# One stage for a kernel's first two layer norms, with the first one's statistics taken in the embedding

## The reference

```python
e  = concat([E_k[id_k] for k in 6 tables])          # (B, S, 96)
h0 = e @ w_eff.T + b                                # (B, S, 64)
h  = layer_norm(h0) * L0_tok_gamma + L0_tok_beta    # first norm, kept as the state
x  = (h - mean(h)) / sqrt(var(h) + 1e-5)            # second norm, input of the attention
h  = h + attention(x, Wq, Wk)
...
```

## Time and profile before

| | us |
|---|---|
| median of 3 runs | 5880.02 (5870.23 to 5885.07) |
| the profiled execution's own time | 5872.68 |
| its span in the profile | 5871.0 |
| PE / DVE / ACT / POOL busy | 4887.5 / 4618.5 / 2553.5 / 2715.3 |

### The profile page before, as it was taken

The page is one execution under the profiler, slowest core; times in us unless marked ns, Lnnn a source line. Parts: engine busy times, 40 slices in busy tenths (PEclk is TensorE's granted clock), DMA queues, the critical chain, the costliest instruction groups (busy, mean ns, idle before and its releaser), DMA issues. The chain is left out here.

```text
span 5871.0 us, 108850 instructions
## 1 busy us (share of the span) xinstructions
PE 4887.5 (83%) x39862; PEld 3314.3 (56%) x39929; DVE 4618.5 (79%) x8619; ACT 2553.5 (43%) x4620; POOL 2715.3 (46%) x3089
## 2 busy tenths in 40 slices
PE   5476977888739999998799999999993679948998
PEld 3463225665525666665677777777772228842452
DVE  7896998998568888886588888888885767767667
ACT  4353443444536666666233333333331442223332
POOL 0000001000636675885767777777775610016557
PEclk9687998999859999999799999999996889969999
DMA  0300000010221110000122222222221000030252
GB/s 19 87 1 6 8 15 34 17 30 26 82 57 18 22 27 13 2 2 9 31 41 44 44 44 44 44 44 44 44 45 21 8 2 3 3 76 22 78 129 42
DMA packets 262988, 195.45 MB, mean 33 GB/s; under 512 B 136426, under 2 KB 239763, under 8 KB 261427
## 3 DMA queue, kind: packets, MB, share of 16 engines
q1 hardware_dynamic: 189662, 132.54, 8.1%
q0 software_dynamic: 72912, 57.02, 6.8%
q10 hardware_dynamic: 12, 0.39, 0.0%
HBM read 113.55 MB, written 69.40 MB: 31 GB/s over the span
## 5 line engine op out<-in xcount | busy, mean ns | idle before, releaser
L3642 PE MATMUL edges_bank<-part_room,hot_room 128*128 128x512 f32 x6656 | 1528.6, 391 | 77.6 <-ACT XT L3665 57.2
L3642 PEld LDWEIGHTS edges_bank<-part_room,hot_room 128*128 128x128 f32 x6656 | 1249.5, 188 | 356.8 <-ACT XT L3665 69.5
L3621 POOL DMA_INDIRECT XT<-gat_node_table,edges_idx x1216 | 1203.1, 989 | 392.4 <-issue 309.6
L3665 ACT COPY XT<-edges_bank 128x512 f32<-128x512 f32 x832 | 475.6, 598 | 657.1 <-PE edges_bank L3642 565.4
L3760 DVE COPY_PREDICATED XT<-edges_tabs_p,XT 128x1024 f32<-128x1024 int32 (+7 forms) x768 | 576.7, 751 | 38.3 <-DVE edges_tabs_p L3733 7.0
L3741 DVE TENSOR_SCALAR hot_room<-edges_lanes,edges_nodes 128x512 fp32r<-128x512 f16 (+1 forms) x768 | 350.8, 518 | 171.6 <-PE edges_bank L3642 86.2
L583 POOL TENSOR_TENSOR X<-H,ln_f_mean 128x1024 f32<-128x1024 f32 x4 | 11.4, 2846 | 877.2 <-DVE ln_f_shift L620 877.2
L1915 ACT ACTIVATE GT<-attc_sc,attc_nm 128x256 f32<-128x256 f32 x1024 | 400.3, 481 | 31.0 <-DVE attc_nm L1993 31.0
L1993 DVE TENSOR_REDUCE attc_nm<-attc_sc 128x4 f32<-128x1024 f32 x256 | 313.0, 1223 | 109.2 <-PE attc_sc L1834 109.2
L1929 ACT ACTIVATE GT<-attc_sct 128x1024 f32<-128x1024 f32 x256 | 262.3, 1025 | 303.2 <-PE attc_sct L1845 303.2
L1834 PE MATMUL attc_sc<-XT,attc_tT 64*128 64x256 f32 x2048 | 295.0, 407 | 44.6 <-ACT GT L1915 44.5
(11 more groups left out here) (869 smaller groups left out, 10077.6 us busy)
## 6 DMA issues: line engine op xcount, KB each, us to landing
gat_states<-GT SPq DMA_DIRECT2D x32, 768.0 KB, 3.4
XT<-gat_node_table,edges_idx POOLq DMA_INDIRECT x1216
edges_lanes<-gat_places SPq DMA_DIRECT2D x128, 128.0 KB, 3.1
expert_pairs<-in_L_ffn_W_dram SPq DMA_DIRECT2D x48, 256.0 KB, 4.3
edges_lanes<-gat_places SPq DMA_DIRECT2D x64, 160.0 KB, 3.3
XT<-XT SPq DMA_DIRECT2D x32, 256.0 KB, 2.4
XT<-XT SPq DMA_DIRECT2D x64, 128.0 KB, 2.0
sorted_in<-stats SPq DMA_DIRECT2D x1, 5568.0 KB, 33.9
```

The costliest lines, as they stand in the source:

```text
L3621: nc.gpsimd.indirect_dma_start(out=rows[:, k, c, :], out_offset=None, in_=q.t_table, in_offset=bass.IndirectOffsetOnAxis(ap=idx[:, k, c:c ...
L3642: m = nc.tensor.matmul(banks[t][:], hot[:, (k * GROUPS + j) % 2, b, t, :], parts[:, p, b].rearrange("p u c -> p (u c)"), start=b == 0 and ...
L3665: nc.scalar.copy(fetched[:, (k * GROUPS + j) % 2, t].rearrange("p u c -> p (u c)"), banks[t][:]).then_inc(fetched_in, 1)
```

## The change

In `embed`, `measure(i)` takes `bn_stats` of the four tiles of step i into `g.stats`, two steps behind the one-hot of the same pass (LAG = 2). The call of `ln_tok` goes, and `layernorm` is replaced by one stage, `entry_norms`, with eight groups of 16 tiles:

- The first norm, in place in `g.H`: groups 1, 2, 4, 5 and 7 by ScalarE (16 activations of 128 x 64 each, `x * rstd + shift`), groups 0, 3 and 6 by VectorE in two operations.
- VectorE applies gamma and beta to every group, takes `bn_stats` of its 16 tiles, and works out moments for two groups at a time.
- The second norm, into `g.X`: groups 0 to 3 by ScalarE, 4 to 7 by VectorE.
- `xs` gets groups 0 to 5 by DMA from SyncE's queue (each 128 x 16 pieces of 64 floats, written at a pitch of 65 floats), groups 6 and 7 by ScalarE.
- TensorE transposes the groups in order 0 to 7 through four PSUM buffers. ScalarE copies out 0 to 4 and 6, VectorE 5 and 7.

```diff
@@ embed, VectorE
+                def measure(i):
+                    v.wait_ge(z_read, i + 1)
+                    for t in range(4 * i, 4 * i + 4):
+                        m = vec.bn_stats(g.stats[:, t, :], g.H[:, t, :])
+                    m.then_inc(measured, 1)
+                    if i == NI - 1:
+                        v.wait_ge(measured, NI)
...
                     if i:
                         collect(i - 1)
+                    if i >= LAG:
+                        measure(i - LAG)
                 collect(NI - 1)
-                v.wait_ge(z_read, NI)
+                for i in range(NI - LAG, NI):
+                    measure(i)
@@ the new stage, entry_norms
+    HT, QT, BUFS = 16, 32, 4
+    FIRST_ACT, FIRST_DVE = (1, 2, 4, 5, 7), (0, 3, 6)
+    THEN_ACT, THEN_DVE = (0, 1, 2, 3), (4, 5, 6, 7)
+    OUT_ACT, OUT_DVE = (0, 1, 2, 3, 4, 6), (5, 7)
+    COPY_DMA, COPY_ACT = (0, 1, 2, 3, 4, 5), (6, 7)
+    xn = g.X
...
+            def _(sp):
+                sp.dma_start(gam[:], gamma.partition_broadcast(P)).then_inc(params, 16)
+                sp.dma_start(bet[:], beta.partition_broadcast(P)).then_inc(params, 16)
+                g.order.load(sp, edges)
+                for n in COPY_DMA:
+                    wait_normed(sp, n)
+                    sp.dma_start(to[:, group(n), :], xn[:, group(n), :]).then_inc(copied, 16)
+                sp.wait_ge(copied, 16 * len(COPY_DMA))
...
+            def _(v):
...
+                def close(n):
+                    s = group(n)
+                    link(vec.tensor_tensor(g.H[:, s, :], g.H[:, s, :], bc(gam[:], 1, HT), ALU.mult))
+                    link(vec.tensor_tensor(g.H[:, s, :], g.H[:, s, :], bc(bet[:], 1, HT), ALU.add))
+                    for t in range(n * HT, (n + 1) * HT):
+                        m = vec.bn_stats(g.stats[:, t, :], g.H[:, t, :])
+                    link(m)
...
+                moments(0, slice(0, TILES)).then_inc(var_ready, 1)
                 v.wait_ge(std_ready, 1)
+                scales(0, slice(0, TILES)).then_inc(scaled, 1)
+                v.wait_ge(params, 32)
+                for n in range(NG):
+                    if n in FIRST_ACT:
+                        v.wait_ge(normed_first, FIRST_ACT.index(n) + 1)
+                    else:
+                        link(norm(0, n, g.H[:, group(n), :]))
+                    close(n)
+                    if n % 2:
+                        moments(1, quarter(n // 2)).then_inc(var_then, 1)
+                    if n in (4, 6, 7):
+                        scales_then((4, 6, 7).index(n))
...
+                v.wait_ge(scaled_then, 3)
+                norm(1, 4, xn[:, group(4), :]).then_inc(normed_v, 1)
+                norm(1, 5, xn[:, group(5), :]).then_inc(normed_v, 1)
+                scales_then(3)
+                v.wait_ge(scaled_then, 4)
+                norm(1, 6, xn[:, group(6), :]).then_inc(normed_v, 1)
+                norm(1, 7, xn[:, group(7), :]).then_inc(normed_v, 1)
+                out(5)
+                out(7)
...
+            def _(act):
...
+                root(0, slice(0, TILES), std_ready)
+                act.wait_ge(scaled, 1)
+                for n in FIRST_ACT:
+                    norm(0, n, g.H, normed_first)
+                    if n in (4, 7):
+                        root_then((4, 7).index(n))
+                norm_then(0)
+                root_then(2)
+                norm_then(1)
+                norm_then(2)
+                root_then(3)
+                out(0)
+                out(1)
+                norm_then(3)
+                for n in (2, 3, 4):
+                    out(n)
+                for n in COPY_ACT:
+                    wait_normed(act, n)
+                    nc.scalar.copy(to[:, group(n), :], xn[:, group(n), :])
+                    if n in OUT_ACT:
+                        out(n)
...
+            def _(pe):
+                for n in range(NG):
+                    wait_normed(pe, n)
+                    if n >= BUFS:
+                        pe.wait_ge(out_a, n - BUFS + 1)
+                    for m in range(HT // 2):
+                        t = nc.tensor.transpose(pt[n % BUFS][:, m * P:(m + 1) * P],
+                                                xn[:, n * HT + 2 * m:n * HT + 2 * m + 2, :].rearrange("p m d -> p (m d)"), g.ident[:])
+                    t.then_inc(turned, 1)
@@ attn0
-        layernorm(nc, g, "ln_a0", g.H, keep=xs[:, :, 0:D], transposed=True, packed=True,
-                  room=g.X[:, 0:TILES // 4, :].rearrange("p (k t) d -> p k t d", k=2))
+        entry_norms(nc, g, I["L0_tok_gamma"], I["L0_tok_beta"], I["L2_ffn_edge_index"], xs[:, :, 0:D])
@@ forward
-            layernorm(nc, g, "ln_tok", g.H, I["L0_tok_gamma"], I["L0_tok_beta"], keep=g.H, edges=I["L2_ffn_edge_index"])
```

More of the change, by code:

```diff
@@ L298, in _ @@
                     t.then_inc(z_full, 1)
[L301 to L318, removed]
-        with nc.Block() as block:
[L320 to L337, removed]
@@ new lines, in entry_norms, with group, wait_normed, quarter @@
+def entry_norms(nc, g, gamma, beta, edges, to):
+    HT, QT, BUFS = 16, 32, 4
+    NG, NQ, N2 = TILES // HT, TILES // QT, D // 2
+    FIRST_ACT, FIRST_DVE = (1, 2, 4, 5, 7), (0, 3, 6)
[3 more added lines that the diff above has]
+    xn = g.X
+    with Stage(nc, "entry") as st:
+        mean, var, std, rstd, shift, gap = (st.sb(n, [P, 2, TILES]) for n in ("mean", "var", "std", "rstd", "shift", "gap"))
+        gam, bet = st.sb("gamma", [P, D]), st.sb("beta", [P, D])
+        pt = [st.ps(f"pt{k}", [P, HT // 2 * P]) for k in range(BUFS)]
+        (params, own, var_ready, std_ready, scaled, normed_first, var_then, std_then, scaled_then, normed_a, normed_v, turned, out_a,
+         out_v, copied) = (st.sem(n) for n in ("params", "vec_own", "var_ready", "std_ready", "scaled", "normed_first", "var_then", "std_then",
+                                       "scaled_then", "normed_a", "normed_v", "turned", "out_a", "out_v", "copied"))
+        def group(n):
+            return slice(n * HT, (n + 1) * HT)
+        def wait_normed(eng, n):
+            if n in THEN_ACT:
+                eng.wait_ge(normed_a, THEN_ACT.index(n) + 1)
+            else:
+                eng.wait_ge(normed_v, THEN_DVE.index(n) + 1)
+        def quarter(q):
+            return slice(q * QT, (q + 1) * QT)
+        def place(n):
+            return g.XT[:, n * (HT // 2) * P:(n + 1) * (HT // 2) * P]
+        with nc.Block() as block:
+            @block.sync
+            def _(sp):
[6 more added lines that the diff above has]
+                sp.wait_ge(copied, 16 * len(COPY_DMA))
@@ L342, in _ @@
                 link = chain(v, own)
[L344 to L351, removed]
@@ L361, in _ @@
[L361 to L368, removed]
@@ L369, in _, with moments @@
[L369 to L386, removed]
+                def moments(k, s):
+                    m, x, d = mean[:, k, s], var[:, k, s], gap[:, k, s]
+                    even, odd = g.stats[:, s, 1], g.stats[:, s, 4]
+                    vec.tensor_tensor(m, even, odd, ALU.add)
+                    vec.tensor_tensor(x, g.stats[:, s, 2], g.stats[:, s, 5], ALU.add)
+                    link(vec.tensor_tensor(d, even, odd, ALU.subtract))
+                    vec.tensor_scalar(m, m, 0.5, None, ALU.mult)
+                    link(vec.tensor_tensor(d, d, d, ALU.mult))
+                    return vec.scalar_tensor_tensor(x, d, N2 / 2, x, ALU.mult, ALU.add)
@@ new lines, in scales, with norm @@
+                def scales(k, s):
+                    link(vec.reciprocal(rstd[:, k, s], std[:, k, s]))
+                    return vec.scalar_tensor_tensor(shift[:, k, s], mean[:, k, s], -1.0, rstd[:, k, s], ALU.mult, ALU.mult)
+                def norm(k, n, to):
+                    s = group(n)
+                    link(vec.tensor_tensor(to, g.H[:, s, :], bc(mean[:, k, s], 2, D), ALU.subtract))
+                    return vec.tensor_tensor(to, to, bc(rstd[:, k, s], 2, D), ALU.mult)
+                def close(n):
+                    s = group(n)
+                    link(vec.tensor_tensor(g.H[:, s, :], g.H[:, s, :], bc(gam[:], 1, HT), ALU.mult))
[3 more added lines that the diff above has]
+                    link(m)
@@ L388, in _ @@
+                out(5)
+                out(7)
             @block.scalar
             def _(act):
-                act.wait_ge(var_ready, 1)
[L391 to L408, removed]
@@ new lines, in norm, with root_then, norm_then @@
+                def norm(k, n, to, done):
+                    for t in range(n * HT, (n + 1) * HT):
+                        m = nc.scalar.activation(to[:, t, 0:D], g.H[:, t, :], ACT.Identity, bias=shift[:, k, t:t + 1],
+                                                 scale=rstd[:, k, t:t + 1])
+                    m.then_inc(done, 1)
+                def root_then(q):
+                    act.wait_ge(var_then, q + 1)
+                    root(1, quarter(q), std_then)
+                def norm_then(n):
```

(2 more changed lines are left out.)

36 lines of the change are left out of this document (15 added, 21 removed).

## The result

| | us |
|---|---|
| before, median of 4 runs beside it | 5878.42 (5870.23 to 5885.07) |
| changed, median of 4 runs | 5852.71 (5842.89 to 5853.59) |
| ratio | 0.9949, 95% interval 0.9935 to 0.9964 |
| changed, profiled execution / its span | 5853.59 / 5851.9 |

What follows compares the result with a forecast made beforehand. VectorE was seen working through two norms almost alone, then three engines taking turns. New stage 74.0 for 108.2 us (-34.2), embedding +2.0, together -32.2: 5840.5 us for the profiled execution, 5847.8 us against the median; range 5837 to 5864.

Steps and rivals of the forecast that it cites:

- The new stage, -34.2 us: Norm stage behind the embedding: 74.0 us forecast in place of the old stretch's 108.2 us.
- The chain: New stage: VectorE waits for beta until 6.1 us; second-norm scales of groups 2 and 3 (quarter 1) come at 50.1 us.
- Who ends the stage: End of the new stage: SyncE's last copies to xs, after group 3 at 63.4 us, end it at 74.3 us.
- The rival of the doubled pieces: Copies to xs: unaligned pieces cost double, 6.2 us a copy; stage ends at 83.6 us, time 5857 us; chance 0.13.
- the choking copies: Six DMA copies to xs queue up: gain under 17.6 us from 7.5 us a copy, chance 0.09; slower, 0.03.
- the 3.1 us: Price of one 512 KB DMA copy to xs, taken from the `sorted_in` load of 256-byte rows.
- TensorE at the faster pace: New stage: transposes of groups 3 to 7 take 9.2 us at the slow pace, about 7 with three groups fast.
- The rival that had it fast: New stage: transfers hidden and TensorE fast; end at 71.7 us, gain 34.5 us, time 5845.5 us; chance 0.20.
- The embedding, +2.0 us: Statistics moved into the embedding: 1.0 us before two casts, 1.0 us behind the last collect, ordinary steps nothing.
- the rival of a VectorE-bound embedding: Embedding: bn_stats at 0.209 us each lengthens some 28 steps by 0.1 to 0.3 us, about 5 us; chance 0.07.
- the embedding's end 2 us later: Expected sign in the new profile: embedding ends 2 us later, its step still 2.39 us.
- if the step of the embedding grew: Sign that would show the prediction wrong: an embedding step longer than 2.39 us.

Runs made afterwards that it cites:

- Run 8: Changed kernel with gamma and beta loaded in the embedding and group 3 of the first norm on ScalarE; median 5850.47 us, ratio 0.9946 to the kernel before.
- Run 9: Changed kernel with all eight copies to xs made by ScalarE, none by DMA; one execution, 5839.87 us, no ratio.
- Run 6: Changed kernel with the ids cast in 32 pieces of 512 columns, one a step; median 5845.32 us, ratio 0.9947 to the kernel before.

## Why the prediction was right

- *The new stage, -34.2 us.* Measured -34.25 in the first two profiles. With the second profile of each kernel, 108.3 before and 75.1 after, it is 33.2 to 34.25, so the agreement to a tenth is luck and the one to a microsecond is not. (The working's latest end was 74.3, yet the sum took 74.0 without a reason; by 74.3 it is -33.9.) The chain ran where the working put it: beta, VectorE's loop, quarter 1's scales, group 3 on ScalarE, TensorE in order. Run 8 took two pieces out of it and got 4.2 of 5.15 us, up to where ScalarE's own work became the bound. ScalarE's idle time, 6.3 us, was 4.85 + 1.50.
- *Who ends the stage.* The copies to `xs`, as said, at T = 73.9 with 0.7 us for the barrier taken off, against 74.3. Two terms of this step were mis-sized and made up for each other, which is luck. A copy takes 2.4 us and not 3.1. And issue and landing, put at 1.5 us together, are about 1.3 us before the first bytes (group 3 is ready at 197.80, and no DMA engine is busy before 199 us) and 1.7 us after the last. The rival of the doubled pieces is refuted by the rows at 202 to 208 us, and with it the choking copies. Run 9 shows that the DMA copies are worth 2.6 us, so they earn little, and cost nothing.
- *Where the 3.1 us came from.* From 5568 KB in 33.9 us, issue to landing. That time holds a wait. In the profile before the rows were issued at 5207.47 us, and 1636 of the 3015 packets from 5207.5 to 5213.9 us were still of 512 bytes or more, loads issued ahead of them. Once only pieces of 256 bytes moved, they moved faster than 168 GB/s. The first row is the kernel before in that stretch, the second the load of the edge numbers in the new stage of the changed kernel (columns of the earlier trace rows):

```profile
5218.00:5236.00 18.00, 11.69 (x110) 11.58 (x110) 5.96 (x4) 0.09 (x1) 0.00 (x0) 0.50 0.96 219
```

```profile
140.00:142.00 2.00, 0.00 (x0) 0.00 (x0) 1.34 (x2) 2.00 (x7) 0.00 (x0) 0.50 1.00 423
```

At 219 GB/s 512 KB take 2.4 us, the time measured for a copy. So the trace of the kernel before did hold the right price, in the GB/s of that stretch and not in the time to landing.

- *TensorE at the faster pace.* 6.10 us for the five groups, under both ends that I gave (7 and 9.2). The other nine profiles of changed kernels have 6.07 to 7.53 us, by when the clock rises, so the faster end of the forecast was the right one. The rival that had it fast was right in that half. It changed nothing, since the transfers end last.
- *The embedding, +2.0 us.* At the same path of the clock 2.05 us: 1.02 from the product at 41.99 us (42.21 in run 9) to the loop's last at 114.05 (115.29), with the two casts in between, and 1.03 behind it, as worked out. The ordinary step is 2.39 us in both kernels: its idle time does cover four bn_stats, and the rival of a VectorE-bound embedding is refuted. Run 6 puts 0.34 us more into the step and lengthens it by 0.11, so the cover is as thin as worked out.
- *What was missing.* No term of the sum and no rival held that TensorE's clock can fall inside the embedding. The sentence that failed is "the embedding's end 2 us later" in what the new profile would show: it came 16.9 us later. That is 2.05 for the statistics, 3.7 for a rise of the clock that came later at the start (a product at 48.09 where one stood at 44.38), and 6.4 + 4.8 for the two falls. The same failure touches the sign "if the step of the embedding grew": it grew to 4.49 us for some steps, by the clock and not by VectorE. The range held the time all the same. The forecast for the profiled execution, 5840.5, missed by 13.1 us. The one for the median missed by 4.9, as it was set against a median 7.3 us above a profile without a fall. One profile of each kernel has falls, so both medians likely hold some; that the two about cancel is argued, not measured, and is luck as far as the prediction goes. Counted over the nine profiles with the casts as they were, 6 of 18 casts at steps 10 and 18 were followed by a fall: 3 of 8 at pauses of 1.23 and 1.38 us, 3 of 10 at 1.73 and 1.88. That the measures make them likelier is not shown. Why a pause of the same length is followed by a fall in one execution and not in the next stays open.

The Trainium skill's page "TensorE: Matmul & The Clock Gate" (Part 1: The HAM clock gate) says that the clock follows how busy TensorE has been of late, and that the same kernel differs from run to run in it. The profiles agree: one kernel, its next stage at 117.57 and at 127.47 us. The Trainium skill's page "DMA: Bandwidth & Descriptors" was cited against this change. By its rule on 256-byte boundaries a copy would have cost 6.2 us in my estimate; measured are 2.4. The section Why small descriptors are slow (HBM only) of the same page of the Trainium skill says that moves within SBUF are spared the penalty of small pieces. This case doesn't bear that out: the copies' 222 GB/s when busy are about half of the 423 GB/s at a share of 1.00 of the edge numbers' load, and no more than the 219 GB/s at 0.96 of the rows to DRAM. Piece length and pitch were not varied, so which of them costs the half is not shown.

## What to carry to other kernels

Work a stage out as a chain over its engines, with the price of each operation from a row, and the transfers as an engine of their own: 34 us were forecast within 1 us here. Take a transfer's price from a stretch in which it moves alone, not from its time to landing. Before a difference between two profiles is put down to a change, look at the granted clock in the stretch and take a second profile of the kernel before: one embedding differed by 9.9 us from itself, and the changed kernel's by 13.3. A long helper operation on a busy loop's feeding engine is a pause for TensorE. Cut into pieces it left no pause and no fall in three profiles, at 0.11 us a step; a gain in the whole time is not shown (medians 5845.32 and 5848.07 us, the changed kernel's 5847.82 and 5852.71).

## What was not expected of the hardware

- Pauses of 1.2 to 1.9 us in TensorE's work, in a loop that otherwise keeps it busy, were followed by a granted clock of 0.50 in 6 of 18 cases. Pauses of 4.05 and 4.20 us were in both. A fall lengthened a step from 2.39 to 4.49 us and cost 3.2 to 6.4 us in the six, and 5.8 and 9.6 us in the two.
- With casts in pieces, three profiles out of three had the clock at 1.00 from 50 to 110 us.
- DMA within SBUF in pieces of 256 bytes, written at a pitch of 260 bytes, ran at 222 GB/s when busy. Rows of 256 bytes that went to DRAM ran at 219 GB/s at a share of 0.96. The load of the edge numbers (two times 1024 KB, 8 KB for each partition) ran at 423 at a share of 1.00.
